# Local attention: the norm's power ahead of the additions, the norms' ends later, the first scores of a block between transposes and values

## The chip, the cores and the metric

The kernel runs on one core of a Trainium2 chip. The metric is the device time of one execution in microseconds, as the median of several runs. The change touches only the first of four stages, the local attention, in the way it orders the instructions of three of the engines: TensorE (PE, matrix products), VectorE (DVE) and GpSimd (POOL). ScalarE (ACT) and the queue that issues the transfers (SyncE, SP) keep their orders.

## The reference, cut to what matters

The whole program is two layers, each an attention and a mixture of experts, on 4096 tokens of width 128. The stage in question is the first attention: 16 heads of width 64, segments of 64 tokens, 16 extra keys and values (pm_k, pm_v) before each segment, and a layer norm over its output that is added to x.

```
xn  = rmsnorm(layernorm(x)) * norm_w
q, k, v = split(xn @ w_qkv);  q, k = rope(q), rope(k)
per segment of 64:  k = [pm_k, k],  v = [pm_v, v]
attn = softmax(mask(q @ k.T * scale));  out = (attn @ v) @ w_out + b_out
x = x + layernorm(out)
```

## The kernel before

The 4096 tokens are cut into 16 blocks of 256 (NSUB), each of two tiles of 128 tokens (s = 0, 1). The work is pipelined over three blocks: in step n, block b = n is projected and its q and k are turned by rope, block a = n - 1 has its softmax and its values, and block z = n - 2 has the values of its second tile, its output projection, and the end of its norm. `steps` has 18 entries: steps 2 to 15 have all three. Each engine runs its own order of calls, written out by hand in one loop over `steps`; semaphores tie them together, so an engine whose next call waits holds all that is behind it.

The parts of a step, with the engine that does each:

- `project(b, i)` (PE): group i of eight (q or k of four heads) into one of two PSUM banks. It waits for the rope products of group i - 2.
- `rope(b, i)` (DVE, L351): two products, of the bank with the sine and the cosine table, into slot i mod 3 of `ma_tr`. It waits for the addition of three groups before, which frees the slot. The sine product is then sent by SP to `ma_swp` in two transfers that swap odd and even rows (L325).
- `add(b, i)` (POOL, L444 for q, L446 for k): adds the cosine product and the swapped one, when the transfers have landed.
- `scores(b, s, j)` (PE, L587 for the mask, L594 for the products): scores of eight heads of a tile; `maxes` (DVE, L358) their row maxima; `exps` (ACT, L495) eight exponentials.
- `softmax_back(a, s)` (DVE): the sums (L365), the reciprocals (L367), then the product for the upper half of the rows (L371). `normalise(a, s)` (POOL) does the lower half (L453) and the part of the extra keys `ma_ppm` (L456).
- `fill(a, s, i)` (PE): transposes of the probabilities (L612), and products with the values (L620), each put back to SBUF by ACT (L505); fill 0 waits for `normalise`. `out_project` (PE, L631 and L634) ends the tile.
- `out_read(a, s)` (DVE, L378 to L385): adds the bias and takes the statistics. `power(a, s)` (POOL, L462): the variance to the power -0.5. `finish(a, s)` (DVE, L390 and L394): applies the norm and adds to X. The second waits for the first.
- `norm(b)` (DVE, L336, twice), `turn` (PE, L551), `high` (ACT, L489) and `low` (DVE, L341) prepare the input of the next block.

A step on PE begins with `fill(z, 1, 0)`, which waits for `normalise` of the step before, and goes on to the values and projections of b. On DVE the order is: `low`, maxima of tile 0, rope 0, `finish(z, 0)`, rope 1, `softmax_back(a, 0)`, ropes 2 and 3, `out_read(z, 1)`, maxima and rope 4, maxima and rope 5, `finish(z, 1)`, ropes 6 and 7, `norm`, `softmax_back(a, 1)`, `out_read(a, 0)`. On POOL: addition 0, `power(z, 0)`, addition 1, `normalise(a, 0)`, additions 2 and 3, `power(z, 1)`, additions 4 to 7, `normalise(a, 1)`.

Of the kernel before, what the change touches and what calls it, by code (L numbers as in the profile page):

```python
# [92 lines left out]
def local_attention(nc, dr, X, g):  # L93

    m = Mem(nc, "a_")
    with m:
# [181 lines left out]
        def tile_of(n, s):  # L278
            return n % 2 * BT + n // 2 * ST + s
# [36 lines left out]
        with nc.Block() as block:  # L316
# [13 lines left out]
            def _(dve):  # L330
# [13 lines left out]
                def rope(b, *gs):  # L344
                    for i in gs:
                        G = b * NG + i
                        dve.wait_ge(proj_mm, G + 1)
                        if G >= TRS:
                            dve.wait_ge(rope_add, G - TRS + 1)
                        for part in (1, 0):  # L350
                            nc.vector.tensor_tensor(tr[:, G % TRS, part, :, :],  # L351
                                                    pbank[:, i % 2, :].rearrange("p (c t) -> p c t", c=2),
                                                    cs[:, b // 2, part, None, :].to_broadcast([P, 2, SUB]),
                                                    ALU.mult).then_inc(rope_mul, 1)
# [32 lines left out]
                def finish(a, s):  # L387
                    T = a * ST + s
                    dve.wait_ge(y_pow, T + 1)
                    nc.vector.tensor_scalar(y[:, s, :], y[:, s, :], ymv[:, s, 0:1], yr[:, s:s + 1],  # L390
                                            ALU.subtract, ALU.mult).then_inc(y_fin, 1)
                    dve.wait_ge(y_fin, T * 2 + 1)
                    xs = X[:, tile_of(a, s), :]
                    nc.vector.tensor_tensor(xs, xs, y[:, s, :], ALU.add).then_inc(y_fin, 1)  # L394

                norm(0)
                for b, a, z, nxt in steps:
                    live, old, older = b is not None, a is not None, z is not None
                    if live:
                        low(b)  # L400
                    if old:
                        maxes(a, 0, 0)
                        maxes(a, 0, 1)
                    if live:
                        rope(b, 0)
                    if older:
                        finish(z, 0)
                    if live:
                        rope(b, 1)
                    if old:  # L410
                        softmax_back(a, 0)
                    if live:
                        rope(b, 2, 3)
                    if older:
                        out_read(z, 1)
                    if old:
                        maxes(a, 1, 0)
                    if live:
                        rope(b, 4)
                    if old:  # L420
                        maxes(a, 1, 1)
                    if live:
                        rope(b, 5)
                    if older:
                        finish(z, 1)
                    if live:
                        rope(b, 6, 7)
                    if nxt is not None:
                        norm(nxt)
                    if old:  # L430
                        softmax_back(a, 1)
                        out_read(a, 0)

            @block.gpsimd
            def _(pool):
                def add(b, *gs):
                    for i in gs:
                        G = b * NG + i
                        kind, c = GROUPS[i]
                        pool.wait_ge(rope_mul, 2 * G + 2)  # L440
                        pool.wait_ge(swapped[G % SWAPS], 32 * (G // SWAPS + 1))
                        t0, t1 = tr[:, G % TRS, 0, :, :], swp[:, G % SWAPS, :, :]
                        if kind == "q":
                            nc.gpsimd.tensor_tensor(qt[:, par(b), 2 * c:2 * c + 2, :], t0, t1, ALU.add).then_inc(rope_add, 1)  # L444
                        else:
                            nc.gpsimd.tensor_tensor(kt[:, par(b), 2 * c:2 * c + 2, :, PM:KEYS0],  # L446
                                                    t0.rearrange("p c (a b) -> p c a b", b=SEG),
                                                    t1.rearrange("p c (a b) -> p c a b", b=SEG),
                                                    ALU.add).then_inc(rope_add, 1)

                def normalise(a, s):
                    pool.wait_ge(rden_done, a * ST + s + 1)
                    nc.gpsimd.tensor_tensor(pb[0:64, s, :, 0:SEG], e[0:64, s, :, PM:KEYS0],  # L453
                                            rden[0:64, s, :, None].to_broadcast([64, H0, SEG]),
                                            ALU.mult).then_inc(p_norm, 1)
                    nc.gpsimd.tensor_tensor(ppm[:, s, :].rearrange("p (h k) -> p h k", k=PM), e[:, s, :, 0:PM],  # L456
                                            rden[:, s, :, None].to_broadcast([P, H0, PM]),
                                            ALU.mult).then_inc(p_norm, 1)

                def power(a, s):  # L460
                    pool.wait_ge(y_chain, (a * ST + s + 1) * 3)
                    nc.gpsimd.tensor_tensor(yr[:, s:s + 1], yve[:, s:s + 1], eps[:, 0:1], ALU.pow).then_inc(y_pow, 1)  # L462

                nc.gpsimd.memset(pb[:, :, :, :], 0.0).then_inc(zeroed, 1)
                pool.wait_ge(zeroed, 1)
                for b, a, z, nxt in steps:
                    live, old, older = b is not None, a is not None, z is not None
                    if live:
                        add(b, 0)
                    if older:  # L470
                        power(z, 0)
                    if live:
                        add(b, 1)
                    if old:
                        normalise(a, 0)
                    if live:
                        add(b, 2, 3)
                    if older:
                        power(z, 1)
                    if live:  # L480
                        add(b, 4, 5, 6, 7)
                    if old:
                        normalise(a, 1)
# [60 lines left out]
            def _(pe):  # L544
# [93 lines left out]
                for b, a, z, nxt in steps:  # L638
                    live, old, older = b is not None, a is not None, z is not None
                    if older:  # L640
                        fill(z, 1, 0)
                    if live:
                        values_of(b, 0)
                        values_of(b, 1)
                    if older:
                        fill(z, 1, 1)
                    if live:
                        values_of(b, 2)
                        values_of(b, 3)
                        project(b, 0)  # L650
                    if older:
                        fill(z, 1, 2, 3)
                    if live:
                        project(b, 1)
                    if older:
                        fill(z, 1, 4)
                    if live:
                        project(b, 2)
                    if older:
                        fill(z, 1, 5, 6)  # L660
                    if live:
                        project(b, 3)
                    if older:
                        out_project(z, 1)
                    if old:
                        scores(a, 1, 0)
                    if live:
                        project(b, 4)
                    if old:
                        scores(a, 1, 1)  # L670
                    if live:
                        project(b, 5)
                    if old:
                        fill(a, 0, 0)
                    if live:
                        project(b, 6)
                    if old:
                        fill(a, 0, 1)
                    if live:
                        project(b, 7)  # L680
                    if old:
                        fill(a, 0, 2, 3, 4, 5, 6)
                        out_project(a, 0)
                    if nxt is not None:
                        turn(nxt)
                    if live:
                        scores(b, 0, 0)
                        scores(b, 0, 1)


# [1752 lines left out]
```

## Time and profile before

| | us |
|---|---|
| median of 3 runs | 2481.97 (2480.72 to 2484.28) |
| the profiled execution | 2475.36 |
| its span | 2473.6 |
| PE busy | 2078.5 (84%) |
| DVE busy | 1605.4 (65%) |
| ACT busy | 999.2 (40%) |
| POOL busy | 655.3 (26%) |

The span runs from the first to the last instruction of the profiled execution. "Busy" is the time in which an engine worked on an instruction, and "idle" time is given with what ended it. The local attention takes up the first quarter of the span. A timeline row gives the start of an instruction (or of several merged ones) in us from the start of the span, its duration, the engine, the line of the kernel, the output and the inputs, the count (x), and in brackets the idle time in front of it with what ended it. Records of neighbouring operations on one engine overlap a little, so the distance of two starts is the better measure of what an operation costs.

### The profile page before, as it was taken

The page shows a single profiled execution, that of the slowest core. Times are in us where ns is not written, and L with a number is a line of the kernel's source. Part 1 is how long each engine was busy: PE and PEld are TensorE (multiplying, and loading weights), DVE is VectorE, ACT ScalarE, POOL GpSimd, SP SyncE. Part 2 cuts the span into 40 slices and gives each one's busy share as a digit, 9 for nine tenths or more (in the row PEclk, how much of TensorE's full clock was granted, in tenths as well). Part 3 has the DMA queues.
Part 4 walks back from the last instruction along what each step waited for, and adds up shares of the span by engine and source line. Part 5 has one row for each costly group of instructions (what it writes and reads, how often), then busy time and mean ns, then how long its engine had stood idle before and what let it go on. Part 6 is the DMA issues. An engine that isn't in the chain of part 4 may idle for free. (4 is left out here: it accounts for less than half of the span.)

```text
span 2473.6 us, 46736 instructions
## 1 busy us (share of the span) xinstructions
PE 2078.5 (84%) x16920; PEld 1650.4 (67%) x16920; DVE 1605.4 (65%) x4182; ACT 999.2 (40%) x1990; POOL 655.3 (26%) x409
## 2 busy tenths in 40 slices
PE   4888888884799988999768885889689869999998
PEld 3667767664456655666556774678477758888887
DVE  5776676774777737777377678677767775333344
ACT  2455455453155552555432222233223334444443
POOL 3545545543145551555400003000300010000000
PEclk9999999997599996999889998899899969999999
DMA  4111111111000000000000001000000020000000
GB/s 154 70 69 58 61 63 65 65 69 36 0 1 2 1 1 1 1 2 1 1 1 0 0 0 41 1 1 1 1 1 1 1 79 5 4 4 4 4 4 8
DMA packets 34795, 54.88 MB, mean 22 GB/s; under 512 B 7104, under 2 KB 16960, under 8 KB 33856
## 3 DMA queue, kind: packets, MB, share of 16 engines
q1 hardware_dynamic: 34624, 52.57, 5.8%
q8 instruction: 111, 1.82, 0.3%
q14 instruction: 60, 0.49, 0.1%
HBM read 16.90 MB, written 2.10 MB: 8 GB/s over the span
## 5 line engine op out<-in xcount | busy, mean ns | idle before, releaser
L1051 POOL TENSOR_TENSOR mb_psum<-mb_pt 128x1024 f32<-128x1024 f32 x112 | 267.1, 2387 | 313.5 <-ACT mb_pt L1031 312.8
L1031 ACT ACTIVATE mb_pt<-mb_stb 128x1024 f32<-128x1024 f32 x256 | 249.2, 1021 | 146.7 <-PE mb_stb L1132 146.2
L2332 PEld LDWEIGHTS md_bk<-md_w,md_a 128*128 128x128 f32 x2048 | 264.0, 192 | 26.2 <-ACT md_a L2179 3.9
L2179 ACT ACTIVATE md_a<-md_bk,md_b 128x512 f32<-128x512 f32 x256 | 175.5, 687 | 244.9 <-PE md_bk L66 244.5
L919 DVE TENSOR_REDUCE mb_mxp<-mb_p1b 128x1 f32<-128x512 f32 x352 | 231.1, 683 | 65.9 <-PE mb_p1b L1116 62.0
L2332 PE MATMUL md_bk<-md_w,md_a 128*128 128x128 f32 x2048 | 267.9, 276 | 2.7 <-DVE md_acc L2276 2.1
L2276 DVE SCALAR_TENSOR_TENSOR md_acc<-md_bk,md_gate,md_acc 128x128 f32<-128x128 f32 x256 | 71.9, 344 | 235.9 <-PE md_bk L2332 235.8
L351 DVE TENSOR_TENSOR ma_tr<-ma_pbank,ma_cs 128x512 f32<-128x512 f32 x256 | 161.6, 682 | 73.3 <-PE ma_pbank L66 69.2
L1955 ACT ACTIVATE mc_p<-mc_sb,mc_nb 128x512 f32<-128x512 f32 (+3 forms) x160 | 98.0, 621 | 186.9 <-DVE mc_nb L1843 186.9
L495 ACT ACTIVATE ma_e<-ma_sbank,ma_mx 128x80 f32<-128x80 f32 x512 | 120.3, 385 | 117.5 <-DVE ma_mx L358 117.5
L2033 PE MATMUL mc_pv<-mc_v,mc_pt 128*128 128x128 f32 x1088 | 149.8, 282 | 11.7 <-DVE mc_pt L1892 11.4
L1116 PE MATMUL mb_p1b<-mb_ks,mb_qs 96*128 96x512 f32 x352 | 152.6, 479 | 6.1 <-DVE mb_qs L912 2.8
L2033 PEld LDWEIGHTS mc_pv<-mc_v,mc_pt 128*128 128x128 f32 x1088 | 134.0, 192 | 23.0 <-DVE mc_pt L1892 18.7
L444 POOL TENSOR_TENSOR ma_qt<-ma_tr,ma_swp 128x512 f32<-128x512 f32 x64 | 88.1, 1378 | 224.3 <-DMA ma_swp<-ma_tr 217.8
L1132 PE MATMUL mb_stb<-mb_qs,mb_ks 98*128 98x512 f32 x512 | 144.7, 404 | 0.8 <-ACT mb_pt L1031 0.8
L1143 PE MATMUL mb_pvb<-mb_pt,mb_v 128*32 128x256 f32 x2048 | 137.0, 385 | 0.0
L64 PE MATMUL md_bk<-md_nh,md_wh 128*128 x256 | 122.9, 480 | 15.2 <-DVE md_acc L2276 12.5
L1516 POOL TENSOR_TENSOR md_frs<-md_fve,md_half 128x4 f32<-128x4 f32 x8 | 8.1, 1007 | 461.8 <-DVE md_fve L1481 461.8
L919 DVE TENSOR_REDUCE mb_mxp<-mb_misc 128x1 f32<-128x512 f32 x160 | 109.1, 682 | 22.0 <-PE mb_misc L1116 22.0
L64 PE MATMUL ma_pbank<-ma_xth,ma_wh 128*128 128x256 f32 x256 | 87.1, 340 | 38.5 <-DVE ma_tr L351 38.4
L1132 PEld LDWEIGHTS mb_stb<-mb_qs,mb_ks 98*128 98x128 f32 x512 | 94.6, 190 | 33.4 <-issue 12.4
L1833 DVE TENSOR_REDUCE mc_mp<-mc_sb 128x1 f32<-128x512 f32 (+3 forms) x160 | 96.6, 609 | 26.1 <-PE mc_sb L2012 13.8
(329 smaller groups left out, 4838.3 us busy)
## 6 DMA issues: line engine op xcount, KB each, us to landing
ma_swp<-ma_tr SPq DMA_DIRECT2D x256, 128.0 KB, 2.0
mg_X<-x SPq DMA_DIRECT2D x4, 512.0 KB, 10.4
ma_cs<-cs SPq DMA_DIRECT2D x1, 2048.0 KB, 9.4
mc_cs<-cs SPq DMA_DIRECT2D x1, 2048.0 KB, 8.1
md_raw<-d_w SPq DMA_DIRECT2D x1, 2048.0 KB, 7.3
md_w<-d_w SPq DMA_DIRECT2D x1, 2048.0 KB, 10.9
out<-mg_X SPq DMA_DIRECT2D x8, 256.0 KB, 2.3
ma_raw<-w_qkv SPq DMA_DIRECT2D x1, 1536.0 KB, 8.4
```

The costliest lines, as they stand in the source:

```text
L64: nc.tensor.matmul(out, lhs_hi, rhs_hi, start=start, stop=False)
L351: nc.vector.tensor_tensor(tr[:, G % TRS, part, :, :], pbank[:, i % 2, :].rearrange("p (c t) -> p c t", c=2), cs[:, b // 2, part, None, :]. ...
L495: nc.scalar.activation(e[:, s, slot, :], sbank[:, 2 * j + k // 4, k % 4 * KEYS0:(k % 4 + 1) * KEYS0], ACT.Exp, bias=mx[:, s, slot:slot + 1 ...
L919: nc.vector.tensor_reduce(mxp[:, r // NCH, r % NCH:r % NCH + 1], pass_bank(r), AXX, ALU.max).then_inc(p1_max, 1)
L1031: nc.scalar.activation(pt[:, T % RING, :, :].rearrange("p (b h) q -> p b (h q)", b=2), stb[:, 2 * (i % 2):2 * (i % 2) + 2, :], ACT.Exp, sc ...
L1051: nc.gpsimd.tensor_tensor(psum[:, n % SUMS, :, :], pt[:, T % RING, :, :], pt[:, (T + 1) % RING, :, :], ALU.add).then_inc(summed, 1)
L1116: nc.tensor.matmul(pass_bank(r), qs[V % 3][0:QROWS, h, t * P:(t + 1) * P], ks[0:QROWS, c * BLK:(c + 1) * BLK], start=True, stop=True).then ...
L1132: last = nc.tensor.matmul(stb[:, 2 * (i % 2) + hp, :], ks[:, i * P:(i + 1) * P], qs[U % 3][:, 2 * hp:2 * hp + 2, :].rearrange("p h q -> p ...
L1143: last = nc.tensor.matmul(pvb[h * DK:(h + 1) * DK, 0:UQ], v1[:, i, :], pt[:, T % RING, h, :], start=(i == 0), stop=(i == KT - 1), skip_gro ...
L2033: last = nc.tensor.matmul(pv[:, 0:D], pt[:, k % 2, a * P:(a + 1) * P], v[:, c * BPT + a, :], start=(c == 0 and a == 0), stop=(c == chunks[ ...
L2179: nc.scalar.activation(a[:, e % 2, c, :], ub[:, c, :], ACT.Gelu, bias=b1[:, e, c:c + 1]).then_inc(gelu, 1)
L2332: last = nc.tensor.matmul(db[:, e % 2, s * P:(s + 1) * P], a[:, e % 2, c, s * P:(s + 1) * P], w2[:, e, c, :], start=(c == 0), stop=(c == F ...
```

## The change

Three orders of calls are altered; no instruction is added or dropped.

- GpSimd: `power(z, 0)` stands ahead of addition 0, and additions 0 and 1 follow each other.
- VectorE: `finish(z, 0)` moves from between ropes 0 and 1 to behind ropes 2 and 3, just ahead of `out_read(z, 1)`. `finish(z, 1)` moves from between ropes 5 and 6 to behind rope 7 and `norm`, just ahead of `softmax_back(a, 1)`.
- TensorE: `scores(b, 0, 0)` moves from behind the transposes of the next block into the fills of block a, between fill 4 (transposes of the probabilities) and fill 5 (products with the values).

```diff
--- before.py
+++ after.py
@@ -402,16 +402,13 @@
                         maxes(a, 0, 0)
                         maxes(a, 0, 1)
                     if live:
-                        rope(b, 0)
-                    if older:
-                        finish(z, 0)
-                    if live:
-                        rope(b, 1)
+                        rope(b, 0, 1)
                     if old:
                         softmax_back(a, 0)
                     if live:
                         rope(b, 2, 3)
                     if older:
+                        finish(z, 0)
                         out_read(z, 1)
                     if old:
                         maxes(a, 1, 0)
@@ -420,13 +417,11 @@
                     if old:
                         maxes(a, 1, 1)
                     if live:
-                        rope(b, 5)
+                        rope(b, 5, 6, 7)
+                    if nxt is not None:
+                        norm(nxt)
                     if older:
                         finish(z, 1)
-                    if live:
-                        rope(b, 6, 7)
-                    if nxt is not None:
-                        norm(nxt)
                     if old:
                         softmax_back(a, 1)
                         out_read(a, 0)
@@ -465,12 +460,10 @@
                 pool.wait_ge(zeroed, 1)
                 for b, a, z, nxt in steps:
                     live, old, older = b is not None, a is not None, z is not None
-                    if live:
-                        add(b, 0)
                     if older:
                         power(z, 0)
                     if live:
-                        add(b, 1)
+                        add(b, 0, 1)
                     if old:
                         normalise(a, 0)
                     if live:
@@ -679,12 +672,15 @@
                     if live:
                         project(b, 7)
                     if old:
-                        fill(a, 0, 2, 3, 4, 5, 6)
+                        fill(a, 0, 2, 3, 4)
+                    if live:
+                        scores(b, 0, 0)
+                    if old:
+                        fill(a, 0, 5, 6)
                         out_project(a, 0)
                     if nxt is not None:
                         turn(nxt)
                     if live:
-                        scores(b, 0, 0)
                         scores(b, 0, 1)
 
 
```

## Rows read from the trace of the kernel before

**Rows 1.** Busy time of PE, PEld, DVE, ACT, POOL in a step; clock, DMA.

```profile
290.61:323.87 33.26, 27.32 (x346) 23.05 (x347) 24.35 (x42) 16.90 (x51) 17.32 (x14) 1.00 0.17 64
```

**Rows 2.** Waits of VectorE, 88 to 556 us: sum, times, longest.

```profile
DVE ma_y L390 <- POOL ma_yr L462: 57.8, 20, 4.1
```

**Rows 3.** Waits of TensorE, the same stretch.

```profile
PE ma_fbank L612 <- POOL ma_ppm L456: 6.9, 13, 1.1
```

**Rows 4.** Timeline of VectorE in this step.

```profile
295.49 1.29 DVE L351 TENSOR_TENSOR ma_tr<-ma_pbank,ma_cs 128x512 f32<-128x512 f32 x2 [3.95 <-PE ma_pbank L66]
300.74 0.35 DVE L390 TENSOR_SCALAR ma_y<-ma_y,ma_ymv,ma_yr 128x128 f32<-128x128 f32 x1 [3.97 <-POOL ma_yr L462]
...
301.33 1.28 DVE L351 TENSOR_TENSOR ma_tr<-ma_pbank,ma_cs 128x512 f32<-128x512 f32 x2
302.53 1.48 DVE L365 TENSOR_REDUCE ma_den<-ma_e 128x16 f32<-128x1280 f32 x1
...
304.33 1.22 DVE L371 TENSOR_TENSOR ma_pb<-ma_e,ma_rden 64x1024 f32<-64x1024 f32 x1
305.58 2.48 DVE L351 TENSOR_TENSOR ma_tr<-ma_pbank,ma_cs 128x512 f32<-128x512 f32 x4
307.98 0.28 DVE L378 TENSOR_TENSOR ma_y<-ma_fbank,ma_bout 128x128 f32<-128x128 f32 x1
...
309.64 1.28 DVE L351 TENSOR_TENSOR ma_tr<-ma_pbank,ma_cs 128x512 f32<-128x512 f32 x2
...
311.57 1.28 DVE L351 TENSOR_TENSOR ma_tr<-ma_pbank,ma_cs 128x512 f32<-128x512 f32 x2
...
314.45 2.47 DVE L351 TENSOR_TENSOR ma_tr<-ma_pbank,ma_cs 128x512 f32<-128x512 f32 x4
...
317.35 1.47 DVE L365 TENSOR_REDUCE ma_den<-ma_e 128x16 f32<-128x1280 f32 x1
...
319.14 2.33 DVE L371 TENSOR_TENSOR ma_pb<-ma_e,ma_rden 64x1024 f32<-64x1024 f32 x1
```

**Rows 5.** Timeline of GpSimd in this step.

```profile
298.94 1.26 POOL L444 TENSOR_TENSOR ma_qt<-ma_tr,ma_swp 128x512 f32<-128x512 f32 x1 [8.38 <-DMA ma_swp<-ma_tr]
...
305.04 1.65 POOL L444 TENSOR_TENSOR ma_qt<-ma_tr,ma_swp 128x512 f32<-128x512 f32 x1 [4.33 <-DMA ma_swp<-ma_tr]
...
313.10 1.28 POOL L444 TENSOR_TENSOR ma_qt<-ma_tr,ma_swp 128x512 f32<-128x512 f32 x1 [0.99 <-DMA ma_swp<-ma_tr]
...
317.89 2.50 POOL L446 TENSOR_TENSOR ma_kt<-ma_tr,ma_swp 128x512 f32<-128x512 f32 x2 [1.63 <-DMA ma_swp<-ma_tr]
320.35 2.88 POOL L453 TENSOR_TENSOR ma_pb<-ma_e,ma_rden 64x1024 f32<-64x1024 f32 x1
```

**Rows 6.** Timeline of TensorE in this step.

```profile
297.49 0.28 PE L66 MATMUL ma_pbank<-ma_xtl,ma_wh 128*128 128x256 f32 x1
...
317.65 1.09 PE L620 MATMUL ma_fbank<-ma_pt,ma_v 128*64 128x128 f32 x16 [0.78 <-ACT ma_pt L505]
...
322.30 0.72 PE L594 MATMUL ma_sbank<-ma_kt,ma_qt 64*64 64x80 f32 x32
...
323.87 0.33 PE L612 MATMUL ma_fbank<-mg_ident,ma_pb 128*128 128x128 f32 x1 [0.16 <-POOL ma_ppm L456]
```

**Rows 7.** Timeline of VectorE in the next step, at its second `finish`.

```profile
346.19 0.35 DVE L390 TENSOR_SCALAR ma_y<-ma_y,ma_ymv,ma_yr 128x128 f32<-128x128 f32 x1
346.57 1.25 DVE L394 TENSOR_TENSOR mg_X<-mg_X,ma_y 128x128 f32<-128x128 f32 x1
```

**Rows 8.** Timeline of GpSimd beside it.

```profile
346.34 1.33 POOL L444 TENSOR_TENSOR ma_qt<-ma_tr,ma_swp 128x512 f32<-128x512 f32 x1 [0.19 <-DMA ma_swp<-ma_tr]
```

**Rows 9.** Timeline of ScalarE, exponentials of tile 0.

```profile
297.65 1.93 ACT L495 ACTIVATE ma_e<-ma_sbank,ma_mx 128x80 f32<-128x80 f32 x8
```

**Rows 10.** Timeline of GpSimd in blocks with a late addition 1.

```profile
272.75 1.28 POOL L444 TENSOR_TENSOR ma_qt<-ma_tr,ma_swp 128x512 f32<-128x512 f32 x1 [5.34 <-DMA ma_swp<-ma_tr]
...
541.75 1.29 POOL L444 TENSOR_TENSOR ma_qt<-ma_tr,ma_swp 128x512 f32<-128x512 f32 x1 [6.26 <-DVE ma_tr L351]
```

## The prediction

> **What bounds the kernel now.** I read the share of each engine by stretch first [rows 1]. A step of the local attention, from one head of TensorE's order to the next, lasts 33.26 us, with TensorE's matrix work at 27.32, VectorE at 24.35, GpSimd at 17.32, and a granted clock of 1.00 (2.4 GHz). No engine is full, so the step is bound by waits. The waits of VectorE [rows 2] show the one that the change aims at: `ma_y L390`, the first operation of `finish`, stands 57.8 us for GpSimd's power, 20 times. TensorE's wait [rows 3] shows how this reaches it: 6.9 us, 13 times, at the head of the step, for the normalised small tile `ma_ppm`.
>
> Then I followed one step on VectorE and on GpSimd [rows 4, 5]. Rope 0 is at 295.49; GpSimd's addition 0 can begin only at 298.94, when the swapped halves have landed; the power goes behind it, and `finish` begins at 300.74 after 3.97 us of idleness. From there VectorE has no gap to the end of softmax_back(a,1), whose last product starts at 319.14 and ends at 321.47. GpSimd's normalisation, which started at 320.35, ends at 323.23, and TensorE starts the next step at 323.87, 0.64 behind it [rows 6]. So the step is this chain: rope 1, softmax_back 0, ropes, softmax_back 1, normalisation. The chance to gain is at most the 3.97 us, times the 14 steps that have both `finish` and live ropes: 56 us.
>
> What one sees on a second look is a collision. The sum of softmax_back 1 is followed by a product of two SBUF tiles (L371), which takes 1.22 us at 304.33 and 2.33 at 319.14, where an addition of GpSimd is running; the normalisation behind it takes 2.88 [rows 4, 5]. It ends 1.08 behind the addition's end (320.39), so it did not begin before. The short operations of `finish` meet the same: at 346.57 the addition to X, otherwise 0.29, takes 1.25, beside GpSimd's addition of 346.34 [rows 7, 8].
>
> **The change part by part**, in the times of that step. I retime each link with the durations of before.
>
> Rope 1 moves ahead. It needs project 1, whose last product ends at 297.49 + 0.28 = 297.77 [rows 6], so it starts at 297.81 instead of 301.33. The sum of softmax_back 0 then is no longer behind VectorE but behind ScalarE: the exponentials of 297.65 end at 299.58 [rows 9], and the sum starts at 299.61 instead of 302.53. That is 2.92 us won so far; 1 us of the stall has turned into another wait.
>
> Addition 1 comes 3.44 us behind the start of its rope (314.45 to 317.89; 309.64 to 313.10 is 3.46 [rows 4, 5]): 301.25, ending at 302.51. The product of softmax_back 0 is due 1.80 behind the sum, at 301.41. Before, it won this race; now it is 0.16 late, waits, and ends at 302.51 + 1.08 = 303.59. The normalisation ends 1.76 behind that, 305.35, and its small tile at about 305.95. Won now: 305.58 - 303.62 = 1.96.
>
> Ropes 2 and 3 take 2.40 (305.58 to 307.98). `finish(z,0)` is moved behind them, at 306.02, just free of GpSimd, and takes the same 0.59 as before (300.74 to 301.33). out_read(z,1) and the first maxima take 1.66, so rope 4 starts at 308.27 instead of 309.64: won 1.37. Rope 5 is 1.93 later, 310.20; rope 6 another 1.20, now with no `finish` between: 311.40. Rope 7 is due at 312.60, but its buffer is free only after addition 4, 308.27 + 3.44 + 1.28 = 312.99: it starts at 313.02. Before it started at about 315.65: won 2.6.
>
> Now the tail. Additions 5, 6 and 7 are due at 313.64, 314.84 and 316.46, with 1.26 each: GpSimd is occupied almost throughout. Against it stand four short operations of VectorE: two of `norm`, then two of `finish(z,1)`. The first comes at 314.22, inside addition 5, and waits until 314.9. When an addition ends, VectorE gets one operation in and the next addition is already waiting; the rows at 346 show that GpSimd gets in between the two halves of `finish` [rows 7, 8]. Whether the second `norm` goes ahead of addition 6 or behind it, addition 7 (from 316.46 to 317.73) ends up ahead of at least the last half of `finish`. So `finish` ends and the sum starts at about 318.3 (317.73 + 0.59), where it was at 317.35: all that was won is gone, and 0.97 more. What comes back is that the product no longer meets an addition: 318.32 + 1.80 = 320.12, + 1.22 = 321.34, normalisation to 323.10, TensorE at 323.74. That is 0.13 us a step better than 323.87.
>
> GpSimd's power itself (0.55 us) ahead of addition 0 costs nothing: GpSimd idles 8.38 us there [rows 5], until the swap lands; the statistics of out_read(z,0) are there from the step before. Queued behind its wait are all additions; none is due before 298.94. If that cover were gone, 0.55 a step.
>
> The scores moved between transposes and values: products of 0.72 us, as at 322.30 [rows 6], and their mask go into a gap of 0.78 in which TensorE waits for ScalarE at 317.65. That takes about 0.7 off TensorE's end of step, and the evacuations there follow the maxima, 1.37 earlier: TensorE is done some 2.1 us sooner, at 321.7, and then waits for the normalisation, 2 us instead of 0.16. Worth 0 as long as GpSimd comes last; at worst the mask and products exceed the gap by 0.2 us, also hidden. Bounds of this edit: 0 to 0.2 lost, and 0.2 won (the wait of 0.16 shows the two were level).
>
> Irregular steps. In 4 of the 14 addition 1 comes 1 to 2 us late (idle 5.34 to 6.26 instead of the 4.33 of this step; the first and the last are in [rows 10]). Then the product of softmax_back 0 is free, but the normalisation runs from 304.3 to 306.2 and its small tile to 306.8, over `finish(z,0)`, which was due at 305.06 and ends at 307.1, 0.5 later than above: these steps lose 0.37 each. The last step with ropes has no `norm`, so `finish` passes one addition earlier: about 1.4 won. Sum: 10 x 0.13 - 4 x 0.37 + 1.4 = 1.2 us won, from bounds per step of -0.9 and +1.8 (below). The two steps without ropes and block 1 have slack on VectorE: 0, at most 0.6 either way each. The profiled execution took 2475.36 us, of which 2473.6 are the span, and the median of the runs is 2481.97; the difference of 6.6 I keep. Forecast: 2474.2 for an execution like the profiled, 2481 for the median.
>
> On the lock there is a rule. The row at 346.19 shows `finish`'s first half lasting to 346.54, and GpSimd's addition starting at 346.34 with 1.33 instead of 1.28: it lost 0.05, not 0.2 [rows 7, 8]. The Trainium skill, "SBUF — State Buffer", section "Who interferes with whom", says that the port pair of VectorE and GpSimd is an exclusive lock held for the full instruction, by a VectorE operation in a 2-port mode or with two SBUF inputs. By that rule each short operation would push additions 6 and 7 by 0.2 more, the step would be 0.27 longer instead of 0.13 shorter, and the sum 2486; by the row it is 2481. The rule on who gets it (first come) and the rows agree.
>
> **The rivals.** (A) VectorE keeps its turn: once let in at 314.9 it does its four short operations in a row. The sum starts at 316.0, addition 7 ends at 318.6, the product at 319.7, TensorE at 322.1: 1.77 won per step, 25 us, 2457. For it: two `norm` operations follow each other without a wait. Against: the rows at 346. (B) No collision matters (GpSimd is done before VectorE comes): everything stays about 3.4 us ahead until TensorE itself bounds, 14 x 3.4 = 48 us, 2434. Against: every such overlap in the trace costs. (C) Slower: the swap transfers. Groups 5, 6 and 7 are now issued within 2.8 us of each other, where before 2.9 us lay between 5 and 6. If landing takes 0.5 us longer, addition 4 holds rope 7 by 0.5 and addition 7 is 1.0 later: the step is 0.87 longer, 12 us, 2494. It decides from 0.07 us of extra landing. For it: the late additions that already occur [rows 10]. Against: groups 6 and 7 were 1.2 us apart before and addition 7 followed 6 without a gap (2.50 for both [rows 5]). (D) The stall does not go (another wait holds `finish` or rope 1): no change, 2482.
>
> **How the numbers follow.** Forecast 0.50, A 0.17, B 0.07, C 0.20, D 0.06. About 5 us (0.2%) is what a measurement of this kernel can tell from no change. Of the forecast's 0.50, 0.34 lie within 0.2%, 0.12 are faster (a jitter of 0.3 us a step is 4 us), 0.04 slower. Faster: 0.12 + 0.17 + 0.07 = 0.36; same 0.34 + 0.06 = 0.40; slower 0.04 + 0.20 = 0.24. The range takes in A and C: 2454 to 2495; the forecast alone would have 2472 to 2489.
>
> **What would show it.** Right: VectorE's wait for `ma_yr` gone, rope 1 some 2.3 us behind rope 0, the sum of softmax_back 0 waiting for ScalarE; L371 of tile 0 longer than 1.22 and that of tile 1 at 1.22; L336, L390, L394 well over 0.35 on average; TensorE's wait for `ma_ppm` at about 2 us a step; the period near 33.1. Wrong: L336 and L390 at their bare times (B), or a period near 31.5 (A), or additions more than 3.6 us behind their ropes (C), or a wait for `ma_yr` that stays (D).

## The result, and the profile after

The changed kernel takes 2455.56 us (median; 2452.74 to 2461.0) against 2483.12 for the kernel before, a ratio of 0.9892 with a 95% interval of 0.9873 to 0.9912: about 27 us, or 1.1%, faster. The forecast was 2481 with a range of 2454 to 2495; the time is at the fast end of that range, near rival A's 2457, and not where the likeliest case put it.

The page of the changed kernel, whose profiled execution took 2461.0 us, the slowest of its four:

```profile
span 2459.2 us, 46736 instructions
...
PE 2072.9 (84%) x16920; PEld 1647.0 (67%) x16920; DVE 1628.2 (66%) x4182; ACT 999.3 (41%) x1990; POOL 666.7 (27%) x409
...
PEclk9999999996699987999879997899799969999999
```

The local attention ends where the statistics of the next stage begin: at 586.5 us instead of 602.7. So this stage is 16.2 us shorter in the pair of profiles, whose spans differ by only 14.4; the later stages take 1.8 us more. The pair shows less than the 27 us between the medians because the profiled execution of the kernel before (2475.36) was 7.8 us under its median and this one is 5.4 over its own.

A step now, with the same columns as in [rows 1], and the waits of VectorE and of TensorE between 88 and 556 us that answer to [rows 2, 3]:

```profile
156.23:188.85 32.62, 27.06 (x346) 23.04 (x346) 25.75 (x42) 16.89 (x51) 18.14 (x15) 1.00 0.17 66
```

```profile
DVE ma_tr L351 <- PE ma_pbank L66: 70.4, 28, 4.4
DVE ma_den L365 <- ACT ma_e L488: 12.7, 15, 5.5
...
DVE ma_tr L351 <- POOL ma_qt L439: 7.3, 14, 1.6
```

```profile
PE ma_fbank L605 <- POOL ma_ppm L451: 15.8, 14, 1.7
```

The wait of `ma_y L390` for GpSimd's power, 57.8 us before, is gone. New are the sum's wait for ScalarE (L365) and short ones of rope 7 for addition 4. TensorE's wait for `ma_ppm` is up from 6.9 to 15.8 us: it is done earlier and waits longer. From the first to the last start of `low` (13 steps) the period is 32.22 us against 33.39 before.

This is the step that begins on TensorE at 156.23. First VectorE, to be read beside [rows 4]:

```profile
161.11 1.29 DVE L351 TENSOR_TENSOR ma_tr<-ma_pbank,ma_cs 128x512 f32<-128x512 f32 x2 [4.42 <-PE ma_pbank L66]
163.43 1.29 DVE L351 TENSOR_TENSOR ma_tr<-ma_pbank,ma_cs 128x512 f32<-128x512 f32 x2 [1.04 <-PE ma_pbank L66]
165.23 1.49 DVE L365 TENSOR_REDUCE ma_den<-ma_e 128x16 f32<-128x1280 f32 x1 [0.51 <-ACT ma_e L488]
...
167.04 2.15 DVE L371 TENSOR_TENSOR ma_pb<-ma_e,ma_rden 64x1024 f32<-64x1024 f32 x1
169.22 2.48 DVE L351 TENSOR_TENSOR ma_tr<-ma_pbank,ma_cs 128x512 f32<-128x512 f32 x4
171.62 0.34 DVE L390 TENSOR_SCALAR ma_y<-ma_y,ma_ymv,ma_yr 128x128 f32<-128x128 f32 x1
...
173.86 1.28 DVE L351 TENSOR_TENSOR ma_tr<-ma_pbank,ma_cs 128x512 f32<-128x512 f32 x2
...
175.79 2.47 DVE L351 TENSOR_TENSOR ma_tr<-ma_pbank,ma_cs 128x512 f32<-128x512 f32 x4
178.69 1.29 DVE L351 TENSOR_TENSOR ma_tr<-ma_pbank,ma_cs 128x512 f32<-128x512 f32 x2 [0.43 <-POOL ma_qt L439]
179.89 1.99 DVE L336 TENSOR_SCALAR ma_xn<-mg_X,ma_mean,ma_xsc 128x128 f32<-128x128 f32 x2
181.80 0.34 DVE L390 TENSOR_SCALAR ma_y<-ma_y,ma_ymv,ma_yr 128x128 f32<-128x128 f32 x1
182.17 1.35 DVE L394 TENSOR_TENSOR mg_X<-mg_X,ma_y 128x128 f32<-128x128 f32 x1
183.45 1.47 DVE L365 TENSOR_REDUCE ma_den<-ma_e 128x16 f32<-128x1280 f32 x1
...
185.24 1.22 DVE L371 TENSOR_TENSOR ma_pb<-ma_e,ma_rden 64x1024 f32<-64x1024 f32 x1
```

then GpSimd, beside [rows 5]:

```profile
164.57 1.26 POOL L439 TENSOR_TENSOR ma_qt<-ma_tr,ma_swp 128x512 f32<-128x512 f32 x1 [7.88 <-DMA ma_swp<-ma_tr]
166.82 1.28 POOL L439 TENSOR_TENSOR ma_qt<-ma_tr,ma_swp 128x512 f32<-128x512 f32 x1 [0.99 <-DMA ma_swp<-ma_tr]
168.06 2.88 POOL L448 TENSOR_TENSOR ma_pb<-ma_e,ma_rden 64x1024 f32<-64x1024 f32 x1
...
177.30 1.28 POOL L439 TENSOR_TENSOR ma_qt<-ma_tr,ma_swp 128x512 f32<-128x512 f32 x1 [1.60 <-DMA ma_swp<-ma_tr]
179.19 1.27 POOL L439 TENSOR_TENSOR ma_qt<-ma_tr,ma_swp 128x512 f32<-128x512 f32 x1 [0.60 <-DMA ma_swp<-ma_tr]
180.51 1.28 POOL L441 TENSOR_TENSOR ma_kt<-ma_tr,ma_swp 128x512 f32<-128x512 f32 x1
182.10 1.27 POOL L441 TENSOR_TENSOR ma_kt<-ma_tr,ma_swp 128x512 f32<-128x512 f32 x1 [0.31 <-DMA ma_swp<-ma_tr]
185.29 2.93 POOL L448 TENSOR_TENSOR ma_pb<-ma_e,ma_rden 64x1024 f32<-64x1024 f32 x1 [1.91 <-DVE ma_rden L367]
```

and the head of the next step on TensorE, beside [rows 6]:

```profile
188.85 0.66 PE L605 MATMUL ma_fbank<-mg_ident,ma_pb 128*128 128x128 f32 x4 [1.62 <-POOL ma_ppm L451]
```

Rope 0 is at +4.88 us from the head as before, rope 1 at +7.20 instead of +10.7, and the sum follows ScalarE with 0.51 of idleness. The product of L371 then meets addition 1 (2.15 us, ending 1.09 behind it), ropes 4 and 5 come at +17.63 and +19.56, and rope 7 waits 0.43 for its buffer. From 179.89 the second `norm` and `finish` meet additions 5, 6 and 7: L336 takes 1.99 for two, L394 1.35. The product of the second tile meets nothing and takes 1.22.

### The profile page after: what moved, and what is told of

It is laid out like the page before. It is cut to its first block and busy times, and to the rows that moved or that the text cites. A ratio compares the mean times of both kernels' runs of the same rounds, so it can differ in the third digit from the quotient of the medians.

```text
span 2459.2 us, 46736 instructions
## 1 busy us (share of the span) xinstructions
PE 2072.9 (84%) x16920; PEld 1647.0 (67%) x16920; DVE 1628.2 (66%) x4182; ACT 999.3 (41%) x1990; POOL 666.7 (27%) x409
## 5 line engine op out<-in xcount | busy, mean ns | idle before, releaser
L64 PE MATMUL md_bk<-md_nh,md_wh 128*128 x256 | 123.1, 481 | 13.9 <-DVE md_acc L2272 12.5
L439 POOL TENSOR_TENSOR ma_qt<-ma_tr,ma_swp 128x512 f32<-128x512 f32 x64 | 82.3, 1289 | 169.5 <-DMA ma_swp<-ma_tr 167.8
L1112 PEld LDWEIGHTS mb_p1b<-mb_ks,mb_qs 96*128 96x128 f32 x352 | 67.5, 199 | 67.1 <-DVE mb_mxp L915 47.9
```

The source lines that it names most:

```text
L64: nc.tensor.matmul(out, lhs_hi, rhs_hi, start=start, stop=False)
L1112: nc.tensor.matmul(pass_bank(r), qs[V % 3][0:QROWS, h, t * P:(t + 1) * P], ks[0:QROWS, c * BLK:(c + 1) * BLK], start=True, stop=True).then ...
```

## The experiments

The kernels were each timed beside the kernel before on the same chip, but not all on one chip: the kernel before had a median of 2483.23 us beside the first four runs below (the three edits alone, and all but the third), 2476.39 beside the next four (all but the second, and the three with operations at the head), and 2480.09 beside the last. So two kernels are compared by their ratios to it; "by the ratios" below is the difference of two ratios times 2483 us. A ratio has an interval of about 0.2% (5 us) to either side, so a difference of two is known to some 6 or 7 us. The period is that of one profile, from the starts of `low` as above.

**The first edit alone.** GpSimd's power and `finish(z, 0)` move, nothing else:

```diff
-                        rope(b, 0)
-                    if older:
-                        finish(z, 0)
-                    if live:
-                        rope(b, 1)
+                        rope(b, 0, 1)
...
+                        finish(z, 0)
                         out_read(z, 1)
```

> Only the first of the three edits: GpSimd's power ahead of the additions and finish(z,0) behind ropes 2 and 3. Theory 1 (the stall goes, port collisions eat part of it): retimed from the trace of before, rope 5 starts 19.6 us into the step instead of 21.0, finish(z,1) meets addition 4, and the product of softmax_back 1 meets addition 6 or 7; period about 32.1 us instead of 33.3, 14 to 18 us faster in all. Theory 2 (the gain of the changed kernel needs its second edit too, which takes finish(z,1) out from between the ropes): about 0 to 5 us faster. Theory 3 (the moved scores make the gain): same time as before.

Measured: 2453.67 us, ratio 0.9883 (0.9860 to 0.9905), mean period 32.09 us. The first edit alone gives all that the whole change gives. Theory 1 had its period right, but its 14 to 18 us was too little for the 29 by the ratio; the profile has the stage end at 584.4 instead of 602.7, 18 us. Theories 2 and 3 fall. The collisions sit where they were expected. VectorE in one of its steps:

```profile
175.07 1.37 DVE L394 TENSOR_TENSOR mg_X<-mg_X,ma_y 128x128 f32<-128x128 f32 x1
...
179.26 1.47 DVE L365 TENSOR_REDUCE ma_den<-ma_e 128x16 f32<-128x1280 f32 x1
...
181.06 2.34 DVE L371 TENSOR_TENSOR ma_pb<-ma_e,ma_rden 64x1024 f32<-64x1024 f32 x1
```

The second half of `finish(z, 1)`, still between the ropes, stands behind addition 4 (1.37), and the product of softmax_back 1 behind an addition (2.34).

**The second edit alone.** `finish(z, 1)` behind rope 7 and `norm`:

```diff
-                        rope(b, 5)
-                    if older:
-                        finish(z, 1)
-                    if live:
-                        rope(b, 6, 7)
+                        rope(b, 5, 6, 7)
                     if nxt is not None:
                         norm(nxt)
+                    if older:
+                        finish(z, 1)
```

> Only the second edit: finish(z,1) behind rope 7 and norm. Theory 1: VectorE still stands for GpSimd's power (about 4 us a step), and now four short operations meet additions 5 to 7, so the sum of softmax_back 1 starts about 1 us later in the step: 0 to 10 us slower. Theory 2: finish(z,1) between the ropes is what holds additions 6 and 7 up, so 8 to 15 us faster.

Measured: 2477.45 us, ratio 0.9973 (0.9960 to 0.9986): 6 to 7 us faster, between the two theories. Both miss: Theory 1 had the wrong sign, Theory 2 too much. Its profile is no help, since in it the period is 33.57 us and the stage ends at 606.8, later than before; a gain of this size does not show in one profile. Why it is faster stays open.

**The third edit alone.** `scores(b, 0, 0)` between fills 4 and 5:

```diff
-                        fill(a, 0, 2, 3, 4, 5, 6)
+                        fill(a, 0, 2, 3, 4)
+                    if live:
+                        scores(b, 0, 0)
+                    if old:
+                        fill(a, 0, 5, 6)
                         out_project(a, 0)
...
-                        scores(b, 0, 0)
                         scores(b, 0, 1)
```

> Only the third edit: scores(b,0,0) between fills 4 and 5. Theory 1: TensorE ends its step 0.7 us earlier but waits for GpSimd's ma_ppm, so no change (within 3 us), and the wait for ma_ppm grows from about 0.5 to about 1.2 us a step. Theory 3: TensorE bounds the head of the step, so 0.7 us a step, 10 us faster.

Measured: 2488.32 us, ratio 1.0015 (0.9999 to 1.0031). No gain, as Theory 1 had it, and Theory 3 falls. In the profile it is worse than nothing (period 34.10 us), and the waits of TensorE between 88 and 556 us, grown from 6.9 to 19.1, show one way how:

```profile
PE ma_fbank L612 <- POOL ma_ppm L456: 19.1, 16, 2.4
...
PE ma_sbank L587 <- POOL ma_kt L446: 5.5, 6, 1.6
```

In the step around 227 us TensorE stands 1.60 us before the scores and 1.46 before fill 0. Busy time of the stretches around the two waits (columns as in [rows 1], the clock is the third number from the end):

```profile
219.00:222.00 3.00, 2.59 (x28) 2.21 (x25) 2.93 (x4) 0.87 (x2) 0.23 (x1) 1.00 0.27 98
222.00:225.00 3.00, 1.40 (x26) 1.19 (x28) 2.16 (x7) 0.38 (x1) 3.00 (x3) 1.00 0.00 0
225.00:228.00 3.00, 1.54 (x40) 1.38 (x30) 0.82 (x1) 0.00 (x0) 1.97 (x2) 0.81 0.00 0
228.00:231.00 3.00, 3.00 (x12) 2.41 (x12) 0.00 (x0) 1.58 (x3) 0.00 (x0) 0.62 0.00 0
```

The clock falls from 1.00 (2.4 GHz) to 0.62 as the mean of the last stretch, so part of it ran at the lower level (1.2 GHz), and rope 0 starts 6.95 us after VectorE's last work instead of 3.98 a step earlier. The Trainium skill, "TensorE: Matmul & The Clock Gate", section "What's actually happening", says that the gate opens with recent activity of the array and closes without it, between 1.2 and 2.4 GHz; the trace agrees in that the fall follows two stretches in which TensorE was busy for 1.40 and 1.54 of 3 us. Between 88 and 556 us the clock falls in seven places in this execution and in three in that of the kernel before (means 0.97 and 0.99). How much of the 34.10 us is due to it is not settled: the swaps were irregular in this execution too.

**All but the third edit** (the same hunk, backward, on the changed kernel):

```diff
+                        scores(b, 0, 0)
                         scores(b, 0, 1)
```

> The changed kernel with scores(b,0,0) back behind the transposes of the next block. Theory 1: GpSimd comes 0.6 to 1.6 us behind TensorE at the head of the step, so taking 0.7 us more of TensorE there costs 0 to 0.3 us a step, 0 to 4 us slower than the changed kernel. Theory 3: it costs 10 us, half of the gain.

Measured: 2459.94 us, ratio 0.9895 (0.9875 to 0.9915), against 0.9892 for the whole change. Worth nothing that can be told, as Theory 1 said.

**All but the second edit** (`finish(z, 1)` back between ropes 5 and 6):

```diff
-                        rope(b, 5, 6, 7)
+                        rope(b, 5)
+                    if older:
+                        finish(z, 1)
+                    if live:
+                        rope(b, 6, 7)
```

> The changed kernel with finish(z,1) back between ropes 5 and 6 (its second edit undone). Theory 1: as with the first edit alone (2454), within 3 us, since at the head of the step GpSimd comes last and the moved scores are worth nothing. Theory 2 (the second edit carries part of the changed kernel's gain): 5 to 15 us slower than the changed kernel.

Measured: 2459.1 us, ratio 0.9914 (0.9894 to 0.9934), period 32.26 us. The ratio lies just above the interval of the whole change (to 0.9912), and the two intervals overlap: by the ratios it is 5 us slower than the changed kernel, the lower end of Theory 2, and 8 slower than the first edit alone, against Theory 1's 3. In the profiles the three are level (the stage ends at 586.8, 586.5 and 584.4). So whether the second edit carries a few us in company with the third is not settled. What it does is a trade: in the mean of 12 steps the last rope ends 24.8 us behind the start of `low` in the changed kernel and 26.3 with the first edit alone, but the sum of softmax_back 1 starts at 28.0 against 26.7, and the product behind it takes 1.22 against 2.13.

**norm at the head of the step.** The changed kernel, with the two operations of `norm` where VectorE and GpSimd both idle:

```diff
                         maxes(a, 0, 0)
                         maxes(a, 0, 1)
+                    if nxt is not None:
+                        norm(nxt)
...
                         rope(b, 5, 6, 7)
-                    if nxt is not None:
-                        norm(nxt)
```

> The changed kernel with norm (two operations that take VectorE's and GpSimd's shared port) moved to the head of the step, behind the maxima of tile 0, where VectorE idles 3.5 us and GpSimd 7.9. Theory 1 (collisions of short operations with additions 5 to 7 set the end of the step): the sum of softmax_back 1 starts near 25.6 us into the step instead of 26.2 to 27.2, period about 31.0 us instead of 32.2, 15 to 20 us faster than the changed kernel; the mean of L336 falls from 1.05 to about 0.33 us. Rival (the swap transfers and additions set the end of the step, and the collisions only fill the waiting): within 5 us of the changed kernel, although L336 gets short.

Measured: 2441.59 us, ratio 0.9853 (0.9832 to 0.9874), period 31.40 us: 10 us under the changed kernel by the ratios (the stage ends at 574.4 instead of 586.5). That is over the rival's 5 and under Theory 1's 15 to 20. Groups of VectorE between 90 and 500 us (count, busy time, mean ns of one):

```profile
L390 DVE TENSOR_SCALAR ma_y<-ma_y,ma_ymv,ma_yr 128x128 f32<-128x128 f32 x26 | 14.7, 565 | 0.0
...
L336 DVE TENSOR_SCALAR ma_xn<-mg_X,ma_mean,ma_xsc 128x128 f32<-128x128 f32 x26 | 7.7, 340 | 0.0
```

`norm` is at 340 ns, and `finish` has taken over its place in the collision: 565 ns on average, where every second of the 26 belongs to tile 1 and stands in the tail. The collision of `norm` is gone. But the move also takes the operations themselves out of the tail, about 0.5 us a step (0.51 from 178.75 to 179.26 with the first edit alone, where nothing meets them) or 7 us in all, and this can explain most of the time by itself. What tells the two apart is the tail: from the end of rope 7 to the start of the sum it takes 3.22 us in the mean of 12 steps of the changed kernel and 1.64 here. Of the 1.58 us less, 0.5 are the two operations and about 1.1 waiting for additions. The period falls by 0.82 us, so not all of it reaches the step.

**finish at the head of the step.** The changed kernel, with `finish(z, 0)` behind the maxima of tile 0, and `finish` of tile 1 one step later, at the same place:

```diff
                         maxes(a, 0, 1)
+                    if z is not None and z > 0:
+                        finish(z - 1, 1)
+                    if older:
+                        finish(z, 0)
...
-                    if older:
-                        finish(z, 1)
```

> The changed kernel with both halves of finish at the head of the step, behind the maxima of tile 0: finish(z,0), and finish of tile 1 one step later than before; norm stays behind rope 7. Theory 1: ropes 4 to 7 start 0.6 us earlier, and only the two operations of norm meet additions; the sum starts near 25.0, TensorE (ready at about 30.1) and GpSimd (30.4) are nearly level, period about 30.4, 22 to 28 us faster than the changed kernel. Rival: within 5 to 10 us of it, from the 0.6 us alone.

Measured: 2433.48 us, ratio 0.9829 (0.9811 to 0.9847), period 30.65 us: 16 us under the changed kernel by the ratios (the stage ends at 563.6), more than the rival's 5 to 10 and less than Theory 1's 22 to 28. The same two groups:

```profile
L336 DVE TENSOR_SCALAR ma_xn<-mg_X,ma_mean,ma_xsc 128x128 f32<-128x128 f32 x26 | 19.4, 787 | 0.0
L390 DVE TENSOR_SCALAR ma_y<-ma_y,ma_ymv,ma_yr 128x128 f32<-128x128 f32 x27 | 9.2, 340 | 0.0
```

Now `finish` is bare (340 ns) and `norm` collides (787 ns). The tail takes 1.41 us. Here too some 1.2 us a step of VectorE's own work have left the stretch between rope 1 and the sum, about 16 us, as much as the gain by the ratios; the collision's share of the time is not separated by this run.

**Both at the head.**

```diff
                         maxes(a, 0, 1)
+                    if nxt is not None:
+                        norm(nxt)
+                    if z is not None and z > 0:
+                        finish(z - 1, 1)
+                    if older:
+                        finish(z, 0)
```

> The changed kernel with norm and both finishes at the head of the step: no short operation meets an addition; only the product of softmax_back 1 meets addition 6. Theory 1: GpSimd is done near 29.8 us, so TensorE's own order bounds the step at 30.1 to 30.3, about 27 to 30 us faster than the changed kernel (near 2427), and TensorE's wait for ma_ppm is gone. Rival: the same as the changed kernel within 10 us, since the additions stay where they are.

Measured: 2433.82 us, ratio 0.9823 (0.9806 to 0.9840), period 30.52 us. By the ratios it is 17 us under the changed kernel (the stage ends at 561.7), between the rival's 10 and Theory 1's 27 to 30, and does not beat the one before it, although the tail is down to nothing: the sum follows rope 7. The waits of VectorE and TensorE between 92 and 500 us say why:

```profile
DVE ma_y L378 <- PE ma_fbank L629: 38.4, 13, 3.4
```

```profile
PE ma_fbank L615 <- ACT ma_pt L500: 24.5, 25, 1.3
...
PE ma_fbank L607 <- POOL ma_ppm L453: 1.1, 4, 0.5
```

VectorE now stands 38.4 us for the output projection, in 13 steps, so it is TensorE that it waits for; and TensorE's wait for `ma_ppm`, 15.8 in the changed kernel, is down to 1.1. What TensorE still waits for is ScalarE's evacuations (24.5) and the ropes (13.9), inside its own order.

**Both at the head, the scores late again.**

```diff
-                        fill(a, 0, 2, 3, 4)
-                    if live:
-                        scores(b, 0, 0)
-                    if old:
-                        fill(a, 0, 5, 6)
+                        fill(a, 0, 2, 3, 4, 5, 6)
                         out_project(a, 0)
...
+                        scores(b, 0, 0)
                         scores(b, 0, 1)
```

> norm and both finishes at the head of the step as in all_head, but scores(b,0,0) back behind the transposes of the next block. Theory 1 (in all_head TensorE's own order bounds the step): the 0.7 us of scores now count, about 0.7 us a step, 8 to 11 us slower than all_head, period near 31.2 us. Rival (GpSimd and VectorE still bound, TensorE has room): the same as all_head within 3 us, as the moved scores were worth nothing in the changed kernel.

Measured: 2439.49 us, ratio 0.9834 (0.9819 to 0.9849), period 31.07 us. In the profiles it is 0.55 us a step, near Theory 1, and the waits of TensorE for ScalarE's evacuations grow, from 24.5 us to:

```profile
PE ma_fbank L615 <- ACT ma_pt L500: 33.2, 37, 1.3
```

The moved scores had filled that gap. By the ratios the price is 0.1%, 3 us, with intervals that overlap, which the rival allows too. The profiles go Theory 1's way; the times do not settle it.

## Why the prediction was right or wrong

**The measured time lay in the range, the likeliest case was wrong.** It said 0.13 us a step, from a retiming link by link; the profiles have 1.17. The time lay in the range because rival A was in it, and A's mechanism is not what happened: that is luck. The retimed step against the one at 156.23 of the changed kernel, in us from its head (in the prediction, from 290.61):

| | predicted | measured |
|---|---|---|
| rope 1 | 7.20 | 7.20 |
| sum of softmax_back 0 | 9.00 | 9.00 |
| its product ends | 12.98 | 12.96 |
| rope 4 | 17.66 | 17.63 |
| rope 5 | 19.59 | 19.56 |
| rope 7 | 22.41 | 22.46 |
| addition 7 starts | 25.85 | 25.87 |
| sum of softmax_back 1 | 27.71 | 27.22 |
| its product starts | 29.51 | 29.01 |
| next step on TensorE | 33.13 | 32.62 |

**The step that failed** is the one in the tail: "So `finish` ends and the sum starts at about 318.3 (317.73 + 0.59)". All the way to addition 7 the times hold to 0.05 us. But the sum came 0.08 us behind the end of addition 7 (182.10 + 1.27 = 183.37, and 183.45), not 0.59. Two things were priced too high. `finish`'s first half stood ahead of addition 7, not behind it: it started at 181.80, because the second `norm`, which waited for addition 6 inside its own record, ended 0.1 us behind it and not a full duration later. And the last half, waiting in the same way, had its 0.29 us nearly all behind it when the addition ended. A blocked operation is not a whole operation to be added after the blocker. The retimed step was 0.5 us too long by this, 7 us over 14 steps.

**A race that I had decided for all steps.** In 4 of 13 steps (31.5 to 31.6 us against 32.3 to 32.7) both halves of `finish` got ahead of addition 7. VectorE and GpSimd in one of them:

```profile
340.74 1.89 DVE L336 TENSOR_SCALAR ma_xn<-mg_X,ma_mean,ma_xsc 128x128 f32<-128x128 f32 x2
342.55 0.33 DVE L390 TENSOR_SCALAR ma_y<-ma_y,ma_ymv,ma_yr 128x128 f32<-128x128 f32 x1
342.92 0.29 DVE L394 TENSOR_TENSOR mg_X<-mg_X,ma_y 128x128 f32<-128x128 f32 x1
343.13 1.48 DVE L365 TENSOR_REDUCE ma_den<-ma_e 128x16 f32<-128x1280 f32 x1
```

```profile
342.96 1.39 POOL L441 TENSOR_TENSOR ma_kt<-ma_tr,ma_swp 128x512 f32<-128x512 f32 x1 [0.41 <-DMA ma_swp<-ma_tr]
```

Here L394 starts at 342.92, the addition at 342.96, so 0.04 us decide that the sum starts at 343.13 and not 1 us later. The prediction had "addition 7 ... ends up ahead of at least the last half of `finish`" without a chance for the other order. It is worth 4 x 1.0 us.

**The late additions.** Four late additions 1 were charged at 0.37 each. In the changed kernel none of 14 was late by a microsecond or more. In the step that ends at 316.95 it came 0.3 late, just behind the product of 295.45, and took 2.26 us instead of 1.28: there the product blocked the addition, and itself took its 1.22. Additions 2 and 3 now come late in several steps (idle up to 2.88 before addition 2), and no rope is seen to wait for them. So the charge stands against nothing in the changed kernel; and the late steps had made the period before 33.39 on average, where the forecast started from 33.26.

Together: 0.13 predicted, 0.5 for the blocked operations, 0.3 for the race, and 0.13 for the mean of before give 1.06 of the measured 1.17 us a step.

**What held.** The stall for the power went; ScalarE took part of its place; the product of softmax_back 0 met addition 1; the tail met three additions; TensorE waited 1.6 us for `ma_ppm` (predicted 2) in 7 of 14 steps, and 0.4 to 1.0 in the others; the scores were worth nothing that can be told, and GpSimd idles 7.88 us behind the power, which was not moved alone. That collisions fill the tail is shown: it takes 3.22 us with four short operations in it, 1.6 and 1.4 with two, nothing with none. What that is worth in time is shown less sharply: `norm` at the head gives 10 us by the ratios, `finish` at the head 16, both 17, and the operations' own durations, which leave the order there too, can account for about 7 and 16 of them. The ends of the stage in the profiles (12 and 23 us earlier) leave some 5 to 7 us for the collisions, the ratios 3 and 0; with 6 to 7 us of uncertainty this is not settled. With both at the head the waits point to TensorE's own order as the next bound.

**The rivals.** A (VectorE keeps its turn) had the time, 2457, but not the mechanism: L394 waits for addition 7 in 9 of 13 steps, and where it does not, addition 6 has held one of the four up. Its mean between 88 and 556 us is 679 ns, against 0.29 us where it is free. The other sum that I gave, 2486 by the Trainium skill's rule ("SBUF — State Buffer", "Who interferes with whom") that the lock is held for the full instruction, charged 0.2 us for each push and was too high: addition 6 starts at +24.28, where the retiming without any push has +24.23, and takes its usual 1.28. Its start of 180.51 lies only 0.03 us inside the record of the first `norm` (to 180.54), so this row does not settle how long the lock is held; the addition of 346.34 [rows 7, 8], which starts 0.20 us inside a `finish` record and loses 0.05, says more against the full duration. That one of the two blocks the other, as the page says, every collision here shows. B (no collision) is what `finish` and `norm` at the head come near, at a period of 30.5 us. C fell: additions 4, 5 and 7 follow their ropes by 3.44, 3.40 and 3.41, as before. D fell: the wait for `ma_yr` is gone.

**Left open.** Of the 27 us between the medians the two profiles show 16 in this stage. The rest would have to be in the scatter between executions, which one profile of each kernel cannot show. What the second edit does beside the others is also open: by itself it is 6 to 7 us faster, and no profile shows why.

## What to carry to other kernels

When two engines block each other, a blocked operation costs the end of the blocker plus a little less than its own duration: 0.1 us for operations of 0.3 here, 1.1 for one of 1.22. With short ones ask how many are caught, not how long they are. Put short operations that need the contended resource where both engines idle, here the head of the step: that was worth 16 to 17 us more, beside the 27 of the change. Try each edit alone: here one of three gave by itself all that the three gave.

## What the runs showed of the hardware

- A short VectorE operation (0.3 us alone) that GpSimd's addition blocks ends 0.1 to 0.15 us behind the addition's end: the second L336 (to 181.88) 0.09 behind the addition of 180.51, L394 0.15 behind that of 182.10. The product of 1.22 us at 167.04 ended 1.09 behind the addition of 166.82. By these rows the part that is left when the block is over is 0.13 to 0.25 us shorter than the whole operation.
- The block goes both ways: in the changed kernel the addition of 295.55, behind the product of 295.45, took 2.26 us instead of 1.28.
- With the third edit alone two waits of 1.60 and 1.46 us close together were followed by a clock of 0.62 over 3 us; the changed kernel's heads at 156.23 and 188.85, with one wait of 1.60 and 1.62, ran at 1.00. The waits alone do not decide it: in the kernel before, waits of 1.30 and 1.02 us (to 100.37 and 102.86) were followed by 0.50 from 103 to 106, and waits of 1.30 and 1.00 (to 300.21 and 302.67) by 1.00 from 303 to 306.
- Late swaps went with the order of the engines' calls: addition 1 started over 4 us behind its rope, instead of 3.4, in 9 of 42 steps of the three profiles without the first edit (4 of 14 in the kernel before), and in none of 112 of the eight with it, with the same transfers. No run tells why.
